# Reading the moving tile and writing PSUM from the last column to the first, in a decoder layer on one core

## Time and profile before

| what | value |
|---|---|
| two runs | 3048.49 and 3055.61 us, median 3052.05 |
| span of the profiled execution, first to last instruction | 3047.5 us |
| PE (TensorE) busy | 2833.3 us, 93% of the span |
| VectorE (DVE), ScalarE (ACT), GpSimd (POOL) busy | 2393.1, 1574.6, 1712.8 us |
| mean granted TensorE clock | 0.971 |

### The profile page before, as it was taken

One profiled execution on the slowest core, in us unless ns is written; L12 is line 12 of the kernel. 1 busy time (PEld: TensorE's weight loads), 2 busy tenths in 40 slices (PEclk: granted clock), 3 DMA queues, 4 the chain that ended last, 5 costly groups with the idle time before them and its releaser, 6 DMA issues. The chain is left out here.

```text
span 3047.5 us, 35696 instructions
## 1 busy us (share of the span) xinstructions
PE 2833.3 (93%) x11958; PEld 2028.4 (67%) x11958; DVE 2393.1 (79%) x2168; ACT 1574.6 (52%) x2685; POOL 1712.8 (56%) x1035
## 2 busy tenths in 40 slices
PE   8997588888788889999999999999989999999997
PEld 7882244444222348888888888887768888887886
DVE  6558999999999977444777777765988888885677
ACT  4448555555665545213888888873433333334443
POOL 0003999999999953403888888861044444430034
PEclk9995799999999999999999999999989999999999
DMA  4228886666875645232111111215245555567654
GB/s 152 83 83 261 274 200 159 179 171 152 250 219 148 199 150 216 104 119 72 37 37 37 37 37 37 71 54 200 97 156 180 180 179 180 180 218 238 194 176 139
DMA packets 217641, 445.84 MB, mean 146 GB/s; under 512 B 33661, under 2 KB 47741, under 8 KB 215613
## 3 DMA queue, kind: packets, MB, share of 16 engines
q1 hardware_dynamic: 179742, 390.73, 41.1%
q10 hardware_dynamic: 37728, 52.96, 5.3%
HBM read 313.45 MB, written 130.15 MB: 146 GB/s over the span
## 5 line engine op out<-in xcount | busy, mean ns | idle before, releaser
L1927 POOL TENSOR_TENSOR at_p_lo<-at_p,at_p_hi 128x512 fp32r<-128x512 f32 x384 | 514.6, 1348 | 244.3 <-ACT at_p_hi L1820 236.5
L716 POOL TENSOR_TENSOR scan_dbx<-scan_u,scan_b_bc 128x1024 f32<-128x1024 f32 x256 | 596.1, 2359 | 0.0
L885 ACT ACTIVATE mamba_ps<-scan_dt,scan_a_neg 128x512 f32<-128x512 f32 (+1 forms) x512 | 332.0, 680 | 315.1 <-DVE scan_g L903 291.3
L914 DVE TENSOR_TENSOR_SCAN mamba_ps<-mamba_ps,scan_dbx 128x1024 f32<-128x1024 f32 x195 | 440.0, 2283 | 3.1 <-ACT mamba_ps L887 1.7
L1847 DVE TENSOR_REDUCE at_neg_max<-heads_ps 128x1 fp32r<-128x1536 f32 x128 | 224.9, 1757 | 134.4 <-PE heads_ps L1939 132.4
L108 PE MATMUL heads_ps<-ff_x_hi,ff_w_hi 128*128 128x512 f32 x784 | 310.0, 395 | 17.2 <-DVE ff_u L2572 6.4
L2812 POOL TENSOR_TENSOR ff_raw<-ff_raw,ff_scale 128x512 f32<-128x512 f32 x112 | 115.9, 1066 | 361.2 <-DMA ff_raw<-in_w 252.8
L109 PE MATMUL heads_ps<-ff_x_lo,ff_w_hi 128*128 128x512 f32 x784 | 308.1, 393 | 0.0
L110 PE MATMUL heads_ps<-ff_x_hi,ff_w_lo 128*128 128x512 f32 x784 | 308.1, 393 | 0.0
L1816 ACT ACTIVATE at_p<-heads_ps 128x512 f32<-128x512 f32 x384 | 228.2, 594 | 110.0 <-PE heads_ps L1963 95.8
L1820 ACT ACTIVATE at_p_hi<-at_p 128x512 fp32r<-128x512 f32 x384 | 242.8, 632 | 12.2
(11 more groups left out here) (306 smaller groups left out, 6906.8 us busy)
## 6 DMA issues: line engine op xcount, KB each, us to landing
scan_dt<-dt SPq DMA_DIRECT2D x120, 256.0 KB, 4.8
scan_u<-u SPq DMA_DIRECT2D x120, 256.0 KB, 7.6
ff_raw<-in_w SPq DMA_DIRECT2D x56, 512.0 KB, 4.6
ff_down_ar<-ac SPq DMA_DIRECT2D x98, 256.0 KB, 2.8
ff_down_hr<-hc SPq DMA_DIRECT2D x98, 256.0 KB, 2.7
ff_act_w<-in_w SPq DMA_DIRECT2D x14, 1024.0 KB, 7.6
hc<-ff_act_t SPq DMA_DIRECT2D x56, 256.0 KB, 6.2
ac<-ff_act_v SPq DMA_DIRECT2D x56, 256.0 KB, 5.9
```

Source lines behind the costliest of these rows:

```text
L716: nc.gpsimd.tensor_tensor(dbx[n % SL][:].rearrange("p (h l) -> p h l", h=2), u[it % 2][:, c:c + 2], b_bc[b][:, k // 2].unsqueeze(1).to_bro ...
L885: nc.scalar.activation(at[:, h * L + h:(h + 1) * L], dt[it % 2][:, c, h:L], ACT.Exp, scale=a_neg[:, it % IT, e:e + 1]).then_inc(a_ready, 1)
L914: nc.vector.tensor_tensor_scan(out[:], ps_a[n % SA], dbx[n % SL][:], 0.0, ALU.mult, ALU.add).then_inc(scanned, 1)
L1927: nc.gpsimd.tensor_tensor(p_lo[n % NSL][:], p[n % NSL][:], f32(p_hi[n % NSL][:]), ALU.subtract).then_inc(p_lo_done, 1)
```

## The change

A helper `back(ap)` gives a view of a two-dimensional operand with its columns in reverse order (a step of -1 from the last element). Three places use it.

- `three_passes` turns its output and both moving tiles round. Column 511 of the moving tile goes through TensorE first and its result is written to column 511 of the PSUM row, then column 510, and so on. Every element ends where it was before. The weight operands are as they were.
- `scores` does the same for its three matmuls.
- `maximum` turns the moving tile alone. The output is still written from the first column to the last, so the row of scores lies in reverse within each bank; the consumer takes only the maximum of a whole row.

No instruction is added, removed or moved on any engine, nor is any wait, semaphore, buffer or DMA: on PE, DVE, ACT, POOL and SP the order of operations and the waits are the same before and after, apart from line numbers.

```diff
+def back(ap):
+
+    return ap[:, ::-1]
+
+
 def three_passes(nc, out, w_hi, w_lo, x_hi, x_lo, start, stop):
 
+    out, x_hi, x_lo = back(out), back(x_hi), back(x_lo)
     nc.tensor.matmul(out, w_hi, x_hi, start=start, stop=False)
     nc.tensor.matmul(out, w_hi, x_lo, start=False, stop=False)
     return nc.tensor.matmul(out, w_lo, x_hi, start=False, stop=stop)
@@ maximum @@
             last = nc.tensor.matmul(ps_mx[:, c], q_hi[hd % NQ][:, i * P:(i + 1) * P],
-                                    k_hi[hd // G % 2][:, c * L:(c + 1) * L], start=True, stop=True)
+                                    back(k_hi[hd // G % 2][:, c * L:(c + 1) * L]), start=True, stop=True)
@@ scores @@
-            nc.tensor.matmul(ps_s[t % 2], k_hi[s][:, c], q_hi[e][:], start=True, stop=False)
-            nc.tensor.matmul(ps_s[t % 2], k_hi[s][:, c], q_lo[e][:], start=False, stop=False)
-            nc.tensor.matmul(ps_s[t % 2], k_lo[s][:, c], q_hi[e][:], start=False, stop=True).then_inc(s_mm, 1)
+            nc.tensor.matmul(back(ps_s[t % 2]), k_hi[s][:, c], back(q_hi[e][:]), start=True, stop=False)
+            nc.tensor.matmul(back(ps_s[t % 2]), k_hi[s][:, c], back(q_lo[e][:]), start=False, stop=False)
+            nc.tensor.matmul(back(ps_s[t % 2]), k_lo[s][:, c], back(q_hi[e][:]), start=False, stop=True).then_inc(s_mm, 1)
```

## The result

The changed kernel takes 3102.88 us (two runs, 3102.34 and 3103.41) against 3052.05: a ratio of 1.0169, 95% interval 1.0139 to 1.0199. It is slower, by 50.8 us. That is inside the range I gave, but it is not the "no change" that I forecast, and the case that I held likeliest did not come. Where a median is quoted, one run stands apart: one of the ten of `e7_base_shifted` took 12183 us at a mean granted clock of 0.614, and the ratios leave it out.

The account below looks back on a forecast made before the run. Float32r matmuls on PE were taken to bound five stages, VectorE the scan; terms 0 + 0 + 0 left the profiled 3047.5 us, a median of about 3052 us, range 3035 to 3180 us.

Parts of the forecast that it names:

- the case that I held likeliest: All changed matmuls keep their rate, 226.7 ns between starts at full clock; time 3052 us, chance 0.75.
- What bounds the kernel: Float32r matmul rate on PE sets nearly everything in five stages; VectorE sets the scan; PE busy 93% of the span.
- It is a fixed cost of each matmul, not of each column: Distance between matmul starts at full clock: 13.3 ns beside one column per cycle, equal at 512 and 384 columns.
- the first rival: Larger fixed cost per matmul: a descending access pays another 13.3 ns at its start; 240 ns distance, 3172 us, chance 0.06.
- Part 1: Backward read of the moving tile, all 9054 matmuls: taken as 0, bounds -13.3 and +200 ns per matmul.
- Part 2: Backward PSUM write, 8670 matmuls, all but the maxima: taken as 0, bounds -13.3 and +200 ns.
- Part 3: ScalarE, VectorE and the maximum wait for the last matmul's semaphore, so column order costs them 0.
- Half rate: Descending read or PSUM write moves one word instead of two, +200 ns per matmul; about 4800 us, chance 0.16.
- The gain: Reverse order avoids the 13.3 ns at the turn between matmuls; at most down to 2932 us, chance 0.03.
- the test that I named: Feed-forward start distance of 226.7, 240 or about 427 to 440 ns; maxima against scores separates read from write; scan unchanged.

Follow-up runs that it names:

- e7_base_shifted: Kernel before, all reads forward, with the base of all SBUF tiles moved by 96 bytes; 3048.13 us against 3049.11, ratio 0.9994.
- e5: Standalone rows of 64 float32r matmuls, varying tile starts, column counts and direction one at a time; 512 columns forward 227.0 ns in place, backward 233.3.
- e6: Standalone rows of 48 matmuls, moving and weight tiles shifted together and apart, three types; float32r shifted together by 64 bytes: 227.1 ns forward, 233.3 backward.
- e10: Standalone rows of 64 float32r matmuls reading the moving tile in blocks, last to first; 64-word blocks 226.9 ns with weights at 0, 233.4 at 64 bytes.
- e1: Changed kernel with PSUM written forwards, moving tiles still read backwards; 3103.31 us against 3048.42 for the kernel before, ratio 1.0183.
- e2: Changed kernel with moving tiles read forwards, PSUM written backwards everywhere, maxima too; 3048.64 us against 3048.42 for the kernel before, ratio 0.9998.
- e11: Changed kernel with back() reversing the order of 64-column blocks, ascending inside each; 3048.76 us against 3047.09 for the kernel before, ratio 1.0004.
- e8: Kernel before, reads forward, with the feed-forward's split weight tiles and what lies behind them starting 64 bytes later; 3072.05 us against 3048.4, ratio 1.0074.

## Why the prediction was wrong

*What bounds the kernel*: right. Nearly every nanosecond of a float32r matmul reached the end. 8862 matmuls at 6.67 ns are 59.1 us, and 192 at 3.8 (177.7 against 173.9 in e5) 0.7; the span grew by 54.6. Of the other 5.2 us, 1.8 are PE idle that shrank; matmuls at the lower clock, which pay nothing, are a part of the rest that I did not count.

*"It is a fixed cost of each matmul, not of each column"*: this reading failed, and the bounds and the price of the first rival were taken from it. The 13.3 ns agreed at 512 and 384 columns in this trace, whose tiles lie well to their weights. Over one column per cycle, 512 columns cost 20.0 ns more in most places and 13.3 where the moving read and the weight tile stand at the same place modulo 256 bytes, on steps of 32 (e5, e6, e10).

*Part 1, the backward read, taken at 0*: this is the step that failed, and it is the whole of the error; the term is 6.67 ns for each matmul of 512 columns, 54.9 us in all by e1 and 50.8 by the change itself. "The same neighbours together as +1, in the other direction" is true, and e10 shows that neighbours are not the point (4-word blocks reversed inside, 226.9 ns); I looked for a price in the order of neighbours and none in how the moving read stands to the weight load beside it. The size lies between my bounds of -13.3 and +200.

*Part 2, the backward write, taken at 0*: right, by e2 (ratio 0.9998) and by the maxima at 233.3 ns. *Part 3, the consumers*: right; in the heads matmuls last 397 ns in place of 389 and PE's idle time before them did not grow.

*The rivals.* The larger cost per matmul, which I gave 0.06, is the one that came: its term was mis-sized, 6.67 ns in place of 13.3, and its reason (a start at the far end of the tile) is not the one; e11 starts at the last block and pays nothing. Half rate did not come in any run with a step of -1. The gain did not come. The first two steps of the test that I named, 233.3 against 226.7 and maxima against scores, did separate read from write before any experiment.

That the time lies in the range is luck: the range reached up to a rival whose reason was wrong, and 1.7% is under the 2% to which I gave 0.75 only because the cost is half that rival's. The middle ground, 1 to 2%, holds a cost of 3 to 7 ns per matmul, and my cases went from nothing to 13.3 ns. I also took 2% to be about what can be told from no change, and would have called the forecast wrong only for a distance moved by more than 7 ns. Both marks were too coarse: the interval is 1.0139 to 1.0199, and the distance moved by 6.7.

## What to carry to other kernels

With float32r matmuls of 512 columns back to back, look at the distance between starts, not at their length, and place the moving tile and the weight tile at the same offset modulo 256 bytes, both at multiples of 32; moving either by 64 bytes costs 2 to 7 ns per matmul of 227. A read from the last column to the first costs 6.7 ns, but in blocks of 64 words it costs nothing, and the write to PSUM may run either way. For other widths measure again: a backward read cost about 4 ns at 384 columns and nothing at 256. A cost that is the same in every row of one trace may be a property of how that kernel is laid out, not of the instruction.

## What was not expected of the hardware

- The distance between float32r matmuls of 512 columns depends on where the weights lie relative to the moving tile: 226.6 to 233.6 ns on steps of 32 bytes, up to 239.8 at starts off a multiple of 16 bytes. With bfloat16 (215.8) and plain float32 (858.3) it does not.
- Fewer weight columns do not help: 32 columns forward take 231.7 ns, 128 columns 226.6.
- At the lower clock neither direction nor place matters: 426.7 ns backward, and in e8 with the weights moved 3.84 / 9 = 426.7 ns too (from 2221.47 to 2225.31 us).
- Blocks of 16 words taken first to last but backwards inside cost 17.07 / 64 = 266.7 ns, the highest of all, while blocks of 4 inside cost nothing and of 64 cost 233.4.

That the two reads disturb each other in SBUF is the simplest reading of a cost that appears when either tile is moved and vanishes when both are. No run shows the mechanism itself, nor why a backward read finds no good place at any of the offsets tried, nor why 256 columns behave otherwise; these stay open.
